# Output bias through a 33-row matmul instead of GpSimd additions in a fused attention and feed-forward kernel

## The chip, the cores and the metric

The kernel runs on one core of one Trainium2 chip. The metric is the device time of one execution in microseconds (us); lower is better. The core has TensorE (PE, with its weight loads shown apart as PEld), VectorE (DVE), ScalarE (ACT), GpSimd (POOL) and SyncE (SP, which issues the DMAs here).

## The reference

```python
# x: (8, 2048, 512); H = 16 heads of DH = 32; M = 128 features
qkv = x @ Wqkv + bqkv                      # q, k, v, split into heads
feature(t) = exp(t @ omega - 0.5 * sum(t * t))
q_prime, k_prime = feature(q), feature(k)
k_v = sum over n of k_prime^T v ; k_sum = sum over n of k_prime
attn = (q_prime @ k_v) / (q_prime @ k_sum + 1e-6)
x = layernorm(x + attn @ Wout + bout)
x = layernorm(x + x @ weight^T + pooled(x) @ disha)
```

All of it is in float32. The change is about `+ bout`, the bias of the output projection, a vector of 512 numbers that is added to every row.

## The kernel before

**Tiles.** The 8 x 2048 rows are worked in 32 chunks of 512 rows, a chunk in 4 tiles of 128 rows. Every large product is made of three float16 products that accumulate in one PSUM bank (high by high, high by low, low by high), so that a projection of one tile is 12 matmuls with a 128-row weight and 512 moving columns. Weights are scaled by WS = 16.

**Pieces.** The work is cut into pieces with two-letter names, and their order on TensorE is written out by hand in strings (`ORDER` for 28 of the 32 chunks, `ORDER_0`, `ORDER_K`, `ORDER_FIRST` ahead, `ORDER_LAST`, `ORDER_Q` behind). KP, VP, QP project keys, values, queries; KN, QN make norms; KF, QF multiply by omega (98-row weights or 98-row moving data); KV sums keys by values; KFIN finishes that sum per batch; NM is the numerator and denominator; AT transposes the attention output; WO is the output projection; YT transposes the normalized rows' input; FF is the feed-forward product; Z writes the result. A piece of 12 matmuls stands in the string in two halves (`WO1.` is the first six, `WO1` the last six), with smaller pieces between. A mark ' means the chunk before. The other engines walk the same strings in their own order: DVE with small lags or by readiness, ACT and POOL in the order in which pieces end.

**Around the change.** SP loads the bias once, spread over 128 partitions, into `bias_out` (L405), and loads the rows of x for tile t into `rows[:, t, :]` once the result that lay there has been stored. GpSimd adds `bias_out` to these rows, 128x512 float32, once per tile (`add_bias`, L958; placed in its order behind the pieces NM0, NM2, QF12 and NM4), and signals `xb_done`. GpSimd also makes rstd and shift of the second layernorm (L969, L972), for which ACT's Z waits. A WO piece: PE waits for `at_hi_done` (ACT's high part of the transposed attention output), then for the bank to be free (`bank_free`, L433), and issues the first six matmuls in `twelve` (L443 to L452); DVE then waits for `wo_done` and `xb_done` and writes rows = bank / 256 + rows (L888), from which the statistics (L770), YT (L610, transposes), ACT's `yt_hi` (L709) and DVE's `yt_lo` (L883) follow. QP, YT and AT share bank_x; WO and FF share bank_y in the long middle.

The stretch of `ORDER` that the prediction speaks of:

```
... AT0 NM2 Z3' KF0 VP1 QF8 NM3 WO0. KF1 QF9 WO0 KV0 KF2 VP2. AT1 KV1 QF10 VP2 QF11
KF3 WO1. QF12 YT0 KV2 QF13 WO1 QF14 QP3. KF4 QF15 ...
```

DVE's subtractions L818 (`k_feat_lo`), L825 (`q_feat_lo`) and L851 (`kv_lo`), the scaling L873 (`attn`) and the addition L866 (`den`) read SBUF only. L883 and L888 read PSUM and SBUF.

Of the kernel before, what the change touches and what calls it, by code (L numbers as in the profile page):

```python
# [22 lines left out]
F32 = mybir.dt.float32  # L23
# [127 lines left out]
def build(nc, xt, x, wqkv, bqk, bv, wout, bout, omega, wffn, disha, out):  # L151
    ctx = ExitStack()
    with ctx:
# [44 lines left out]
        bias_qk = sb("bias_qk", [P, 2 * G], F32)  # L198
        bias_qk16 = sb("bias_qk16", [P, 2 * G], F32)
        bias_v16 = sb("bias_v16", [P, D], F32)  # L200
        bias_out = sb("bias_out", [P, D], F32)
        omega_f = sb("omega_f", [P, M], F32)
        omega_s = sb("omega_s", [P, M], F16)
        norm_w = sb("norm_w", [P, 32], F32)
# [44 lines left out]
        def units(bank):  # L249
# [5 lines left out]
            k_hi k_sq k_lo v_hi_done v_lo_done kn_hi kn_lo k_exp kfl kfin fin_a fin_b fin_l fin_c nm_low nm_sum k_stacked  # L255
            qp_done qn_done qf_done nm_done at_done wo_done yt_done ff_done q_hi q_sq q_lo qn_hi qn_lo
            q_exp qfl q_stacked den_done rec_done normed at_hi_done at_lo_done yt_hi_done yt_lo_done
            xb_done r1_done st1 ag1 floor_done st2 ag2 var2 rstd2 z_done w_sum w_summed bv_scaled w_mean w_even pool_pow
            xt_loaded xt_hi_done xt_lo_done dve_waited sp_waited""".split()
        S = {n: sem(n) for n in names}  # L260
        xk_loaded, wk_loaded = ([sem(f"{s}_loaded{kb}") for kb in range(KB)] for s in ("xk", "wk"))
# [62 lines left out]
        def _(sp):  # L324
# [60 lines left out]
            def step(b, c, kind, i, what):  # L385
                kA, j, jq = 4 * b + c, 4 * b - 4 + c, 4 * b - 3 + c
                if kind == "XT":
                    if kA + 1 < B * CPB:
                        wait(sp, "xt_lo_done", kA)
                        if kA == 0:  # L390
                            wait(sp, "xk_lo", KB)
                        carry()
                        load_xt(kA + 1)
                elif kind == "WL":
                    if kA == 0:
                        sp.dma_start(wq_f[:, :, :], rows_of_w(wqkv, 0)).then_inc(wq_loaded, 16)
                        sp.dma_start(wo_f, rows_of_w(wout, 0)).then_inc(wo_loaded, 16)
                        sp.wait_ge(S["wk_lo"], KB)
                        sp.dma_start(wf_f, rows_of_w(wffn, 0)).then_inc(wf_loaded, 16)
                        for r in range(2):  # L400
                            sp.dma_start(attn[64 * r:64 * (r + 1), :], disha).then_inc(disha_loaded, 16)
                        sp.dma_start(bias_v16[:, :], bv.partition_broadcast(P)).then_inc(bv_loaded, 16)
                        sp.dma_start(bias_out[:, :], bout.partition_broadcast(P)).then_inc(bo_loaded, 16)
                elif kind == "STK":
                    stack_up("k", kA, "k_stacked")  # L405
                elif kind == "NRK":
                    stack_norms("k", kA, "k_stacked")
                elif kind == "STQ":
                    stack_up("q", jq, "q_stacked")
                elif kind == "NRQ":  # L410
                    stack_norms("q", jq, "q_stacked")
                elif kind == "LX":
                    load_x(b, c, i, j)
                elif kind == "ST":
                    store(b, c, i, j)
# [8 lines left out]
        def _(pe):  # L424
# [15 lines left out]
                        wait(pe, name, per * chunk_of(*there, k) + m + 1)  # L440
                        return

            def twelve(bank, parts, what, done, order, low):  # L443

                at = [(kb, *order[m]) for m in range(3) for kb in range(KB)]
                for n in (range(0, 6) if what == "first" else range(6, 12)):
                    if n == 8:
                        wait(pe, *low)
                    lhs, rhs = parts(*at[n])
                    last = nc.tensor.matmul(bank[:, :], lhs, rhs, start=n == 0, stop=n == 11)  # L450
                if what == "last":
                    last.then_inc(S[done], 1)  # L452

# [28 lines left out]
            def step(b, c, kind, i, what):  # L482
# [91 lines left out]
                elif kind == "NM":  # L574
                    t, u = i // 2, i % 2
                    wait(pe, "qfl", 16 * j + 8 * (t // 2 + 1))
                    if i < 2:
                        wait(pe, "kfin", 2 * b - 1 + i)
                    bank = bank_nm_of(b, c, i)
                    if bank is bank_kf:  # L580
                        wait(pe, "k_exp", 16 * B * CPB)
                    if alone(b, c):
                        wait(pe, "nm_sum", 8 * LAST_Q)
                        wait(pe, "normed", 8 * j + max(i - 1, 0))
                    else:
                        wait(pe, "nm_sum", 8 * j + i)
                    for hl in range(8):
                        h = 8 * u + hl
                        hh = G * (h % HPG) + h // HPG
                        pos = slice(P * (t % 2), P * (t % 2 + 1))  # L590
                        at = W1 * hl if alone(b, c) else WN * hl
                        width = WN if hl < WIDE and not alone(b, c) else W1
                        nc.tensor.matmul(bank[:, at:at + width], q_feat_hi[:, hh, pos], kv_both[:, h, 0:width],  # L593
                                         start=True, stop=False, skip_group_check=True)
                        if width == W1:
                            nc.tensor.matmul(bank[:, at:at + W1], q_feat_hi[:, hh, pos], kv_lo[:, h, :],
                                             start=False, stop=False, skip_group_check=True)
                        last = nc.tensor.matmul(bank[:, at:at + W1], q_feat_lo[:, hh, pos], kv_hi[:, h, :],  # L598
                                                start=False, stop=True, skip_group_check=True)
                    last.then_inc(S["nm_done"], 1)  # L600
                elif kind in ("AT", "YT"):
                    if kind == "AT":
                        wait(pe, "normed", 8 * j + 2 * i + 2)
                    else:
                        wait(pe, "r1_done", TPC * j + i + 1)
                    bank_free(b, c, kind, i)
                    src = attn[:, :] if kind == "AT" else rows[:, i, :]
                    bank = bank_of(b, c, kind, i)
                    for kb in range(KB):
                        last = nc.tensor.transpose(bank[:, P * kb:P * (kb + 1)],  # L610
                                                   src[:, P * kb:P * (kb + 1)], ident[:, :])
                    last.then_inc(S["at_done" if kind == "AT" else "yt_done"], 1)
                elif kind in ("WO", "FF"):
                    if what == "first":
                        wait(pe, "at_hi_done" if kind == "WO" else "yt_hi_done", TPC * j + i + 1)
                        bank_free(b, c, kind, i)
                    if j == 0 and i == 0 and what == "first":
                        wait(pe, "wo_lo", KB)
                        wait(pe, "wf_lo", KB)
                    l, r = (at_p[i % 2], wo_p) if kind == "WO" else (yt_p[i % 2], wf_p)  # L620
                    twelve(bank_of(b, c, kind, i), lambda kb, s, m: (l[s][:, kb, :], r[m][:, kb, :]), what,
                           "wo_done" if kind == "WO" else "ff_done", LHS_LOW_LAST,
                           ("at_lo_done" if kind == "WO" else "yt_lo_done", TPC * j + i + 1))

            slots(pe, PE_ORDERS, step)

# [89 lines left out]
        def _(dve):  # L716
# [79 lines left out]
            def step(b, c, kind, i, what):  # L796
# [87 lines left out]
                                    yt_hi[:, u, :, :], ALU.subtract).then_inc(S["yt_lo_done"], 1)  # L884
                elif kind == "WO":
                    wait(dve, "wo_done", n)
                    wait(dve, "xb_done", n)
                    v.scalar_tensor_tensor(out=rows[:, i, :], in0=bank_of(b, c, kind, i)[:, :], scalar=1.0 / WS / WS,  # L888
                                           in1=rows[:, i, :], op0=ALU.mult,
                                           op1=ALU.add).then_inc(S["r1_done"], 1)  # L890
# [24 lines left out]
                elif kind == "WF":  # L915
                    if kA == 2:
                        if i == 0:
                            dve.wait_ge(bv_loaded, 16)
                            v.tensor_scalar(bias_v16[:, :], bias_v16[:, :], WS, None, ALU.mult).then_inc(S["bv_scaled"], 1)
                            dve.wait_ge(wf_loaded, 16)  # L920
                            dve.wait_ge(disha_loaded, 16 * 2)
                            dve.wait_ge(S["pool_const"], 2)
                        sum_w(i)
# [22 lines left out]
        def _(pool):  # L946
# [4 lines left out]
                                    ).then_inc(S["pool_const"], 1)  # L951
            pool.wait_ge(S["dve_const"], 5)

            def add_bias(j, t):
                if j == 0:
                    pool.wait_ge(bo_loaded, 16)
                wait(pool, x_loaded[t], 16 * (j + 1))
                nc.gpsimd.tensor_tensor(rows[:, t, :], rows[:, t, :], bias_out[:, :],  # L958
                                        ALU.add).then_inc(S["xb_done"], 1)

            BIAS_BEHIND = (("NM", 0), ("NM", 2), ("QF", 12), ("NM", 4))

            def step(b, c, kind, i, what):
                kA, j = 4 * b + c, 4 * b - 4 + c
                if kind == "FF":
# [5 lines left out]
                    wait(pool, "pool_pow", TPC * j + i + 1)  # L971
                    nc.gpsimd.tensor_scalar(shift[:, u:u + 1], mean_var[:, 1, u, 0:1], rstd[:, u:u + 1], -1.0,  # L972
                                            ALU.mult, ALU.mult).then_inc(S["rstd2"], 1)
                elif (kind, i) in BIAS_BEHIND:
                    add_bias(j, BIAS_BEHIND.index((kind, i)))

            slots(pool, ENDED, step)

# [32 lines left out]
```

## Time and profile before

| | us |
|---|---|
| median of 3 runs | 2447.77 |
| lowest and highest of them | 2444.79, 2451.57 |
| the profiled execution | 2453.35 |
| its span, first to last instruction | 2451.6 |
| granted TensorE clock, mean over the span | 0.995 of full speed |

The profile is one execution. Its page gives the busy time of each engine, the chain of work that ended last, and the costliest groups of instructions by line. A matmul's end in it is modelled: matmuls that follow each other start closer together than their shown durations, so the distance of starts is what a matmul costs, and a busy TensorE is not one at its peak. For an idle stretch of PE the profile names what ended it.

### The profile page before, as it was taken

The numbers are of one execution on the slowest core, as the hardware profiler recorded it, in microseconds if no ns is written. First come the engines' busy times: TensorE is split into PE (matmuls) and PEld (weight loads), VectorE is DVE, ScalarE is ACT, GpSimd is POOL, SyncE is SP. The second block draws the span as 40 slices with busy tenths as digits, with TensorE's granted clock in tenths as the row PEclk, the third lists the DMA queues.
The fourth block names the chain that finished last, engine by engine and source line by source line (L and its number), as shares of the span: only waits on it lengthen the run. The fifth ranks groups of instructions, "written<-read, shape, count | busy, mean of one in ns | idle before, by whom it ended". The sixth has DMA issues, their size and how long they took to land.

```text
span 2451.6 us, 55233 instructions
## 1 busy us (share of the span) xinstructions
PE 2364.0 (96%) x21224; PEld 1326.1 (54%) x21224; DVE 1984.2 (81%) x4007; ACT 1265.7 (52%) x2281; POOL 291.1 (12%) x390
## 2 busy tenths in 40 slices
PE   8989999999999999999999999999999999998897
PEld 3545555555555555555555555555555555554454
DVE  6777887888888888888888888888887888877776
ACT  4544555555555555555555555555555555554433
POOL 0001111011111011111011111011111011111121
PEclk9999999999999999999999999999999999999999
DMA  6322323323323323323323323323323323221231
GB/s 204 87 69 74 102 70 91 92 77 94 101 69 94 92 72 99 96 64 104 92 68 104 93 65 102 91 72 105 79 79 97 86 81 105 73 68 53 71 91 48
DMA packets 160277, 213.11 MB, mean 87 GB/s; under 512 B 19376, under 2 KB 119824, under 8 KB 156048
## 3 DMA queue, kind: packets, MB, share of 16 engines
q1 hardware_dynamic: 159440, 208.53, 30.7%
q8 instruction: 170, 2.79, 0.5%
q10 hardware_dynamic: 576, 1.05, 0.1%
q14 instruction: 91, 0.75, 0.1%
HBM read 73.19 MB, written 33.55 MB: 44 GB/s over the span
## 4 chain that ended last, share of the span: by engine, by line
PE 61%; DVE 22%; issue 8%; ACT 5%; SPq 1%; POOL 1%; DMA 1%; DVEq 0%; POOLq 0%; ACTq 0%
PE bank_a L450 18%; PE bank_y L450 13%; PE bank_x L450 13%; DVE q_feat_lo L825 3%; DVE k_feat_lo L818 3%; PE bank_qf L569 3%; PE bank_x L610 3%; PE bank_kf L515 2%; DVE xt_lo L938 2%; DVE stats L770 2%; PE kv_ps L541 2%; DVE yt_lo L883 2%; DVE v_both L812 1%; PE bank_nm L593 1%; DVE nm_f L863 1%
## 5 line engine op out<-in xcount | busy, mean ns | idle before, releaser
L678 ACT ACTIVATE k_feat<-bank_kf 128x512 f32<-128x512 f32 x512 | 305.8, 597 | 255.1 <-PE bank_kf L515 223.8
L688 ACT ACTIVATE q_feat<-bank_qf 128x512 f32<-128x512 f32 x512 | 304.9, 595 | 177.1 <-PE bank_qf L569 176.6
L818 DVE TENSOR_TENSOR k_feat_lo<-k_feat 128x512 bf16<-128x512 f32 x512 | 369.6, 722 | 19.5 <-ACT k_feat L678 19.1
L825 DVE TENSOR_TENSOR q_feat_lo<-q_feat 128x512 bf16<-128x512 f32 x512 | 352.5, 695 | 33.2 <-ACT q_feat L688 28.7
L969 POOL TENSOR_TENSOR rstd<-mean_var,minus_half 128x1 f32<-128x1 f32 x128 | 82.8, 647 | 1687.3 <-DVE mean_var L901 1687.3
L958 POOL TENSOR_TENSOR rows<-rows,bias_out 128x512 f32<-128x512 f32 x128 | 165.9, 1308 | 456.3 <-DMA rows<-x 456.3
L515 PE MATMUL bank_kf<-omega_s,stack_k 98*128 98x128 f16 x1920 | 185.9, 219 | 3.4 <-ACT k_feat L678 3.0
L569 PE MATMUL bank_qf<-stack_q,omega_s 98*128 98x256 f16 x960 | 184.4, 273 | 4.1 <-ACT q_feat L688 3.2
L541 PE MATMUL kv_ps<-v_both,k_feat 128*128 128x65 f16 (+1 forms) x2048 | 181.4, 190 | 4.8 <-DVE k_feat_lo L818 4.8
L515 PEld LDWEIGHTS bank_kf<-omega_s,stack_k 98*128 98x128 f16 x1920 | 137.9, 97 | 85.7 <-issue 23.5
L547 PE MATMUL kv_ps<-v_both,k_feat_lo 128*128 128x33 f16 x2048 | 182.7, 179 | 0.0
L541 PEld LDWEIGHTS kv_ps<-v_both,k_feat 128*128 128x128 bf16 x2048 | 154.3, 97 | 48.6 <-DVE k_feat_lo L818 15.1
L781 DVE SCALAR_TENSOR_TENSOR t_lo_k<-bank_a,bias_qk,t_hi_k 128x512 f16<-128x512 f32 x119 | 89.3, 751 | 110.4 <-ACT squares_k L651 110.4
L704 ACT ACTIVATE at_hi<-bank_x 128x512 f16<-128x512 f32 x112 | 66.9, 597 | 206.2 <-PE bank_x L610 206.1
L781 DVE SCALAR_TENSOR_TENSOR t_lo_q<-bank_x,bias_qk,t_hi_q 128x512 f16<-128x512 f32 x128 | 95.8, 749 | 80.2 <-ACT squares_q L651 80.2
L547 PEld LDWEIGHTS kv_ps<-v_both,k_feat_lo 128*128 128x128 bf16 x2048 | 142.6, 96 | 30.8
L450 PE MATMUL bank_y<-wout_lo,at_hi 128*128 128x512 f16 x512 | 153.8, 382 | 0.0
L646 ACT ACTIVATE t_hi_q<-bank_x,bias_qk 128x512 f16<-128x512 f32 x128 | 88.1, 688 | 124.1 <-PE bank_x L450 120.7
L450 PE MATMUL bank_x<-xt_hi,wqkv_hi 128*128 128x512 f16 x512 | 132.8, 382 | 19.9 <-DVE yt_lo L883 19.2
L450 PE MATMUL bank_x<-xt_hi,wqkv_lo 128*128 128x512 f16 x512 | 148.3, 380 | 0.0
L593 PE MATMUL bank_nm<-kv_both,q_feat 128*128 128x66 bf16 (+1 forms) x1920 | 138.8, 188 | 6.6 <-issue 3.6
L598 PE MATMUL bank_nm<-kv_both,q_feat_lo 128*128 128x33 bf16 x1920 | 143.2, 178 | 0.0
(198 smaller groups left out, 5180.5 us busy)
## 6 DMA issues: line engine op xcount, KB each, us to landing
rows<-x SPq DMA_DIRECT2D x128, 256.0 KB, 2.9
out<-rows SPq DMA_DIRECT2D x128, 256.0 KB, 2.0
xt_f<-xt SPq DMA_DIRECT2D x31, 1024.0 KB, 5.1
stack_k<-t_hi_k SPq DMA_DIRECT2D x240, 128.0 KB, 2.4
stack_q<-t_hi_q SPq DMA_DIRECT2D x240, 128.0 KB, 2.4
stack_k<-t_lo_k SPq DMA_DIRECT2D x120, 128.0 KB, 2.4
stack_q<-t_lo_q SPq DMA_DIRECT2D x120, 128.0 KB, 2.4
stack_q<-t_hi_k SPq DMA_DIRECT2D x16, 128.0 KB, 2.4
```

The costliest lines, as they stand in the source:

```text
L450: last = nc.tensor.matmul(bank[:, :], lhs, rhs, start=n == 0, stop=n == 11)
L515: last = nc.tensor.matmul(bank_kf[:, M * jj:M * (jj + 1)], stack_of("k", kA)[0:STACK, g, jj, P * t:P * (t + 1)], omega_s[0:STACK, :], star ...
L541: nc.tensor.matmul(o[:, at:at + width], hi, v_both[:, t, h, 0:width], start=c == 0 and t == 0 and h % 8 == 0, stop=False, skip_group_check ...
L547: last = nc.tensor.matmul(o[:, at:at + W1], lo, v_both[:, t, h, 0:W1], start=False, stop=end, skip_group_check=True)
L569: last = nc.tensor.matmul(bank_qf[:, HALF * e:HALF * (e + 1)], omega_s[0:STACK, :], stack_of("q", j)[0:STACK, hh % G, hh // G, HALF * half ...
L593: nc.tensor.matmul(bank[:, at:at + width], q_feat_hi[:, hh, pos], kv_both[:, h, 0:width], start=True, stop=False, skip_group_check=True)
L678: nc.scalar.activation(k_feat[:, i % 2, :], bank_kf[:, :], ACT.Exp, scale=1.0 / WS).then_inc(S["k_exp"], 1)
L688: nc.scalar.activation(q_feat[:, 2 * pair:2 * pair + 2, :], bank_qf[:, :].rearrange("p (e n) -> p e n", e=2), ACT.Exp, scale=1.0 / WS).the ...
L781: v.scalar_tensor_tensor(out=t_lo[s][:, i, :], in0=bank[:, :], scalar=bias_qk16[:, m:m + 1], in1=t_hi[s][:, i, :], op0=ALU.add, op1=ALU.su ...
L818: v.tensor_tensor(k_feat_lo[:, u, :], k_feat[:, u, :], k_feat_hi[:, u, :], ALU.subtract).then_inc(S["kfl"], 1)
L825: v.tensor_tensor(q_feat_lo[:, at, :], q_feat[:, at, :], q_feat_hi[:, at, :], ALU.subtract).then_inc(S["qfl"], 1)
L958: nc.gpsimd.tensor_tensor(rows[:, t, :], rows[:, t, :], bias_out[:, :], ALU.add).then_inc(S["xb_done"], 1)
```

## The change

The bias enters the accumulation of WO on TensorE. `bias_rows` holds the float16 high part of 16 x bias (computed for 33 partitions at once; row 0 is used) and, in row 32, its low part; `pick` is a 33x128 float16 weight, zero but for rows 0 and 32, which hold 16. One matmul with this weight and 512 columns opens the accumulation of each WO bank, ahead of the twelve, whose first now has start=False. Rows 1 to 31 meet zero weights. PE waits for the free bank first, issues this matmul, and waits for `at_hi_done` behind it. GpSimd's additions and the semaphore `xb_done` are gone; DVE's L888 waits for the load of the rows itself. The set-up of the two tensors (five DVE instructions) is put once into the piece WF0 of chunk 2. The bias is loaded over 33 partitions instead of 128.

```diff
-        bias_out = sb("bias_out", [P, D], F32)
+        bias_out = sb("bias_out", [DH + 1, D], F32)
+        bias_rows = sb("bias_rows", [DH + 1, D], F16)
+        pick = sb("pick", [DH + 1, P], F16)
...
-                        sp.dma_start(bias_out[:, :], bout.partition_broadcast(P)).then_inc(bo_loaded, 16)
+                        sp.dma_start(bias_out[:, :], bout.partition_broadcast(DH + 1)).then_inc(bo_loaded, 16)
...
-            def twelve(bank, parts, what, done, order, low):
+            def twelve(bank, parts, what, done, order, low, begun=False):
...
-                    last = nc.tensor.matmul(bank[:, :], lhs, rhs, start=n == 0, stop=n == 11)
+                    last = nc.tensor.matmul(bank[:, :], lhs, rhs, start=n == 0 and not begun, stop=n == 11)
...
                 elif kind in ("WO", "FF"):
                     if what == "first":
+                        bank_free(b, c, kind, i)
+                        if kind == "WO":
+                            if j == 0 and i == 0:
+                                wait(pe, "bo_lo", 1)
+                                wait(pe, "picked", 3)
+                            nc.tensor.matmul(bank_of(b, c, kind, i)[:, :], pick[:, :], bias_rows[:, :], start=True, stop=False)
                         wait(pe, "at_hi_done" if kind == "WO" else "yt_hi_done", TPC * j + i + 1)
-                        bank_free(b, c, kind, i)
...
                 elif kind == "WO":
                     wait(dve, "wo_done", n)
-                    wait(dve, "xb_done", n)
+                    wait(dve, x_loaded[i], 16 * (j + 1))
...
                             v.tensor_scalar(bias_v16[:, :], bias_v16[:, :], WS, None, ALU.mult).then_inc(S["bv_scaled"], 1)
+                            dve.wait_ge(bo_loaded, 16)
+                            v.tensor_scalar(bias_rows[:, :], bias_out[:, :], WS, None, ALU.mult).then_inc(S["bo_hi"], 1)
+                            dve.wait_ge(S["bo_hi"], 1)
+                            v.scalar_tensor_tensor(out=bias_rows[DH:DH + 1, :], in0=bias_out[DH:DH + 1, :], scalar=WS,
+                                                   in1=bias_rows[DH:DH + 1, :], op0=ALU.mult,
+                                                   op1=ALU.subtract).then_inc(S["bo_lo"], 1)
+                            v.memset(pick[:, :], 0.0).then_inc(S["picked"], 1)
+                            dve.wait_ge(S["picked"], 1)
+                            v.memset(pick[0:1, :], WS).then_inc(S["picked"], 1)
+                            v.memset(pick[DH:DH + 1, :], WS).then_inc(S["picked"], 1)
...
-            def add_bias(j, t):
-                if j == 0:
-                    pool.wait_ge(bo_loaded, 16)
-                wait(pool, x_loaded[t], 16 * (j + 1))
-                nc.gpsimd.tensor_tensor(rows[:, t, :], rows[:, t, :], bias_out[:, :],
-                                        ALU.add).then_inc(S["xb_done"], 1)
-
-            BIAS_BEHIND = (("NM", 0), ("NM", 2), ("QF", 12), ("NM", 4))
...
-                elif (kind, i) in BIAS_BEHIND:
-                    add_bias(j, BIAS_BEHIND.index((kind, i)))
```

## Rows read from the trace of the kernel before

**Rows 1.** The page: span, busy time by engine, and the chain's shares.
```profile
span 2451.6 us, 55233 instructions
...
PE 2364.0 (96%) x21224; PEld 1326.1 (54%) x21224; DVE 1984.2 (81%) x4007; ACT 1265.7 (52%) x2281; POOL 291.1 (12%) x390
...
PE 61%; DVE 22%; issue 8%; ACT 5%; SPq 1%; POOL 1%; DMA 1%; DVEq 0%; POOLq 0%; ACTq 0%
```

**Rows 2.** PE's waits, 282 to 2205 us: waiter, awaited: us in total, times, longest.
```profile
PE bank_x L450 <- DVE yt_lo L883: 16.2, 26, 1.4
PE bank_x L610 <- DVE half_norm L792: 4.8, 26, 0.3
```

**Rows 3.** One line's instructions, whole trace: count: ns min/median/max, first and last start.
```profile
L818 DVE TENSOR_TENSOR k_feat_lo<-k_feat x512: 677/684/1781, 34.3 to 2245.5; 128x512 bf16<-128x512 f32 x171
L825 DVE TENSOR_TENSOR q_feat_lo<-q_feat x512: 674/684/1356, 163.4 to 2423.7; 128x512 bf16<-128x512 f32 x171
L873 DVE TENSOR_TENSOR attn<-nm_f,den x224: 424/425/1351, 186.9 to 2231.5; 128x256 f32<-128x256 f32 x112
L851 DVE TENSOR_TENSOR kv_both<-squares_k,kv_both x16: 432/434/1443, 182.9 to 2255.6; 128x264 bf16<-128x264 f32 x16
L883 DVE TENSOR_TENSOR yt_lo<-bank_x,yt_hi x112: 677/683/693, 207.8 to 2248.3; 128x512 f16<-128x512 f32 x112
L958 POOL TENSOR_TENSOR rows<-rows,bias_out x128: 1261/1272/1727, 187.4 to 2427.0; 128x512 f32<-128x512 f32 x128
```

**Rows 4.** Timeline ahead of QP3, one chunk, POOL, DVE and PE: start us, us.
```profile
1015.02 2.50 POOL L958 TENSOR_TENSOR rows<-rows,bias_out 128x512 f32<-128x512 f32 x2 [5.29 <-DMA rows<-x]
...
1016.49 1.58 DVE L818 TENSOR_TENSOR k_feat_lo<-k_feat 128x512 bf16<-128x512 f32 x1
...
1021.60 0.68 DVE L883 TENSOR_TENSOR yt_lo<-bank_x,yt_hi 128x512 f16<-128x512 f32 x1
...
1021.37 0.38 PE L569 MATMUL bank_qf<-stack_q,omega_s 98*128 98x256 f16 x2
1022.33 1.04 PE L450 MATMUL bank_x<-xt_hi,wqkv_hi 128*128 128x512 f16 x4 [0.58 <-DVE yt_lo L883]
```

**Rows 5.** The same place in another chunk, with the longer stall.
```profile
498.78 1.59 DVE L818 TENSOR_TENSOR k_feat_lo<-k_feat 128x512 bf16<-128x512 f32 x1
...
500.90 1.15 DVE L825 TENSOR_TENSOR q_feat_lo<-q_feat 128x512 bf16<-128x512 f32 x1
...
505.11 1.04 PE L450 MATMUL bank_x<-xt_hi,wqkv_hi 128*128 128x512 f16 x4 [1.24 <-DVE yt_lo L883]
```

**Rows 6.** Timeline of PE and PEld, an ordinary WO: full-speed distances, weights of two heights.
```profile
1010.06 1.02 PE L450 MATMUL bank_y<-wout_hi,at_hi 128*128 128x512 f16 x4
...
1010.92 0.59 PE L450 MATMUL bank_y<-wout_lo,at_hi 128*128 128x512 f16 x2
...
1011.35 0.39 PE L515 MATMUL bank_kf<-omega_s,stack_k 98*128 98x128 f16 x4
```

**Rows 7.** Timeline of the tail: a WO that waits for ACT's at_hi.
```profile
2234.07 1.04 PE L450 MATMUL bank_y<-wout_hi,at_hi 128*128 128x512 f16 x4 [0.40 <-ACT at_hi L704]
```

**Rows 8.** Timeline of DVE and PE, first attention output: AT0 waits.
```profile
191.38 1.20 DVE L873 TENSOR_TENSOR attn<-nm_f,den 128x256 f32<-128x256 f32 x1
...
192.64 0.66 PE L610 MATMUL bank_x<-ident,attn 128*128 128x128 f32 x4 [2.61 <-DVE attn L873]
```

**Rows 9.** Timeline of PE behind a batch's KFIN: NM1 inside FF3.
```profile
485.36 0.59 PE L450 MATMUL bank_y<-wffn_lo,yt_hi 128*128 128x512 f16 x2
486.02 0.19 PE L593 MATMUL bank_nm<-kv_both,q_feat 128*128 128x66 bf16 x1
```

**Rows 10.** Timeline of DVE at the piece WF0 of chunk 2.
```profile
76.51 0.42 DVE L919 TENSOR_SCALAR bias_v<-bias_v 128x512 f32<-128x512 f32 x1
...
79.00 0.75 DVE L781 SCALAR_TENSOR_TENSOR t_lo_k<-bank_a,bias_qk,t_hi_k 128x512 f16<-128x512 f32 x1 [0.55 <-ACT squares_k L651]
...
80.72 0.69 DVE L736 SCALAR_TENSOR_TENSOR wout_lo<-q_feat,wout_hi 128x512 f16<-128x512 f32 x1
```

More of the change, by code:

```diff
@@ L257, in build @@
             q_exp qfl q_stacked den_done rec_done normed at_hi_done at_lo_done yt_hi_done yt_lo_done
-            xb_done r1_done st1 ag1 floor_done st2 ag2 var2 rstd2 z_done w_sum w_summed bv_scaled w_mean w_even pool_pow
+            bo_hi bo_lo picked r1_done st1 ag1 floor_done st2 ag2 var2 rstd2 z_done w_sum w_summed bv_scaled w_mean w_even pool_pow
             xt_loaded xt_hi_done xt_lo_done dve_waited sp_waited""".split()
@@ L622, in step @@
                            "wo_done" if kind == "WO" else "ff_done", LHS_LOW_LAST,
-                           ("at_lo_done" if kind == "WO" else "yt_lo_done", TPC * j + i + 1))
+                           ("at_lo_done" if kind == "WO" else "yt_lo_done", TPC * j + i + 1), kind == "WO")
             slots(pe, PE_ORDERS, step)
```

## The prediction

> **What bounds the kernel now.** I read the page first. TensorE is shown busy for 96% of the span and carries 61% of the chain that ended last, VectorE 22% [rows 1]; GpSimd is busy for 12% and has about 1% of the chain. So TensorE's time is the time, and what is left to win are its stalls. GpSimd's 128 additions of some 1.27 us each [rows 3] are not on the chain themselves. The second view, TensorE's waits in the 26 even chunks of the middle, shows what VectorE costs it: 16.2 us in 26 waits of bank_x for `yt_lo`, one a chunk, and 4.8 us in 26 waits for `half_norm` [rows 2]. The third view, durations of single lines, tells why VectorE may be late: a line that reads SBUF alone has a median of 684 ns but a maximum of 1781 or 1356 ns, `attn` 425 against 1351, `kv_lo` 434 against 1443, while `yt_lo`, which reads PSUM and SBUF, keeps to 677 to 693 [rows 3]. The timeline says with what these slow ones coincide. Two additions ran as a pair from 1015.02 for 2.50 us; `k_feat_lo` began at 1016.49 in the second of them and took 1.58 us, 0.90 over its median. VectorE works without a pause from there to `yt_lo`, which ends at 1022.28, and QP3 begins at 1022.33 [rows 4].
>
> How long TensorE really stood: full-speed matmuls of 512 columns start 0.215 us apart (four in 1010.92 - 1010.06 = 0.86 [rows 6]), so the two 256-column matmuls of QF14 at 1021.37 were through at 1021.59, and the stall was 0.74 us, 0.16 more than the 0.58 shown, because the shown end is modelled [rows 4].
>
> **Part by part, and the sum.** The sum is made against the profiled execution of 2453.35 us (span 2451.6), which lies 5.6 above the median of 2447.77; I add the sum to the median.
>
> *Added matmuls.* 128 of them, one per tile, 512 moving columns each. At 0.215 each [rows 6] that is 27.5 us on an engine that has hardly a hole, so all of it is on the path. Its waits change places but ask for nothing that is later than before: the bank was awaited in the same place. Queued behind this earlier wait are only the WO matmuls, which need the bank anyway. The trace has no 33-row weight. Nearest is the 98-row one, whose four 128-column matmuls take 0.23 us from 1011.35 [rows 6] to the next piece: the same rate per column, with no seam at the change from 128 rows to 98. So I take 0.215. Bounds: zero, if a matmul this thin ran beside its neighbour, and 0.38 us, the shown duration of one alone, 49 us in all. Where TensorE waits for ACT's high part the new matmul slips into the wait; rows show that in the tail (0.40 us [rows 7]), and I credit one such place, -0.2.
>
> *Against a page.* The matmuls of [rows 6] follow one another at 0.215 us although each has a weight of its own, so those loads are hidden. The Trainium skill ("TensorE: Matmul & The Clock Gate", Part 3, "The mechanism") says that a weight load overlaps with matmuls in flight only when its row group differs. Strictly by that rule no load here would be hidden; the trace does not agree with it. It is taken up again in the second rival.
>
> *GpSimd's additions gone, at QP3.* What they took from VectorE there is larger than the stall: 0.90 us against 0.74 [rows 4]; in the chunk with the long stall 0.91 + 0.47 = 1.38 against 1.24 + 0.16 = 1.40 [rows 5]. A stall that goes up and down with the excess is made by it. Besides, the new matmul of WO1 stands between WO0, from which `yt_lo` descends, and QP3, and so gives VectorE 0.215 us more. So the whole stall goes: 16.2 + 26 x 0.16 = 20.4 us, and 0.8 (an estimate, the mean of these) for the 27th chunk of this kind, outside the stretch: -21.2. Bounds: 0 and -21.2. What is late next there is QF15, which needs ACT's exponential of QF14, and that moves up with QF14.
>
> *In other places.* The first attention output: `attn` took 1.20 for 0.425, and AT0 waited 2.61 us for it [rows 3, 8]: -0.8. NM1 behind KFIN, seven times: `kv_lo` up to 1.443 for 0.434 [rows 3]; two matmuls from 485.36 were through at 485.79, NM1 began at 486.02 [rows 9], so 7 x 0.23 = -1.6. Bounds of the two: 0 and -2.4.
>
> *Set-up.* Five VectorE instructions behind L919: a scaling (0.42), a subtraction as dear as L736 (0.69, since it has as many columns) and three memsets, together put at one more scaling (0.42, an estimate): 1.5 us. VectorE idles 0.55 us soon behind that place [rows 10], and more later, so most is hidden by TensorE's queued projections; if that cover is gone it costs 1.5. I take +0.5. The smaller bias load, the missing semaphore and VectorE's wait for the rows' load itself I cost at nothing: the addition could start only when the rows had landed, at 1015.02 [rows 4], so what L888 waits for now comes 1.3 us or more before what it waited for.
>
> *Sum:* 27.5 - 0.2 - 21.2 - 0.8 - 1.6 + 0.5 = **+4.2 us**; 2447.8 + 4.2 = **2452.0 us** (the profiled execution would be 2457.6). In other words, 110 of the 128 matmuls lie in the middle and give back almost exactly what the additions cost there; the end pays.
>
> **The rivals.**
> (1) *The stall at QP3 stays*, because VectorE or ACT is late for another reason and the slow `k_feat_lo` only hides it, or because the slow instructions are not GpSimd's doing. Then +4.2 + 21.2 = +25.4, 2473 us. It decides if QP3 still starts more than 0.3 us behind QF14. Against it: the two chunks of [rows 4, 5]. Chance 0.09.
> (2) *Each new matmul shows its weight load.* One seam or two more per tile: a wait stands on either side of the matmul, and what is loaded behind a wait is not always loaded ahead. I bound a seam by the 0.16 us between a matmul's own columns and its shown end: 128 x 0.1 to 128 x 0.16 is +13 to +20 on top, 2465 to 2472 us. It decides if the distance from this matmul to the first of WO is over 0.3 us. Against it: WO's first half already stands behind two waits and follows its forerunner with no seam [rows 6]. The skill's rule named above is what would make it so. Chance 0.11.
> (3) *VectorE's relief reaches farther.* It works up to 1.4 us less per chunk, and the 4.8 us of waits for `half_norm` (9 with the 0.16 each) [rows 2] may go too, with some of the 2.6 us at AT0. Then -9 - 2, 2441 us. Against it: these waits are 0.3 at the longest in every chunk, however long QP3 had stalled in it [rows 2], so VectorE has caught up by then. Chance 0.14.
> (4) *The thin matmul is nearly free*: -20 or so, 2430 us. No row speaks for it, since 98 rows cost what 128 cost. Chance 0.02.
> My own case has 0.64.
>
> **How the numbers follow.** A change under 0.3%, 7.3 us, cannot be told from none in this kernel. My case lies at +4.2 with terms that can miss by some 5 either way, so about 0.09 of its 0.64 is beyond +7.3 and 0.01 beyond -7.3; rival (3), at -6.8, falls on both sides of the bound. Faster 0.12: 0.09 of rival (3), 0.02 of rival (4), 0.01 of mine. Slower 0.29: rivals (1) and (2) with 0.20, and 0.09 of mine. Same 0.59: 0.54 of mine and 0.05 of rival (3). The range: down to 2442, which takes in rival (3) nearly, and up to 2466, the lower end of rival (2).
>
> **What would show it.** Right: GpSimd's L958 gone; `k_feat_lo` and `q_feat_lo` with maxima near 0.7 us; the waits of bank_x for `yt_lo` down from 26 to a few; 128 new bank_y matmuls 0.215 us apart from their neighbours; the chunk's period changed by 0.1 us. Wrong: new waits of PE on the free bank ahead of the new matmul; seams around it; a wait at QP3 of the old size; a period that grew by 0.8 us, or shrank.

## The result, and the profile after

The changed kernel takes 2475.65 us (median of 4 runs, 2473.32 to 2479.97) against 2449.18 us before (median of 4 runs by then): ratio 1.0118, 95% interval 1.0105 to 1.0131, 26.5 us slower. The forecast was 2452.0 us, within 2442 to 2466; it was too low by 24 us, and outside its range. The two profiled executions lie 20 us apart (2453.35, the slowest of its kernel, and 2473.32, the fastest of its own), so sums made from the traces come out smaller than the 26.5 us between the medians.

The page of the changed kernel:

```profile
span 2471.5 us, 55236 instructions
...
PE 2406.3 (97%) x21352; PEld 1339.7 (54%) x21352; DVE 1944.2 (79%) x4012; ACT 1265.3 (51%) x2281; POOL 125.1 (5%) x262
...
PE 78%; DVE 10%; issue 4%; ACT 4%; SPq 2%; POOL 1%; DMA 1%; DVEq 0%; POOLq 0%; ACTq 0%
```

Against [rows 1]: VectorE's share of the chain fell from 22% to 10%, TensorE's rose from 61% to 78%. That is what the forecast wanted of GpSimd's going. TensorE's waits in its even middle (waiter, awaited: us in total, times, longest):

```profile
PE bank_x L612 <- DVE half_norm L799: 4.4, 26, 0.2
PE bank_nm L595 <- issue: 3.6, 6, 0.6
```

The line that led in [rows 2], 16.2 us of waits for `yt_lo`, is gone altogether. The slow VectorE instructions of [rows 3] are gone too, with maxima now beside the medians (count: ns min/median/max):

```profile
L825 DVE TENSOR_TENSOR k_feat_lo<-k_feat x512: 678/684/694, 34.0 to 2260.7; 128x512 bf16<-128x512 f32 x171
L832 DVE TENSOR_TENSOR q_feat_lo<-q_feat x512: 679/684/697, 161.7 to 2442.7; 128x512 bf16<-128x512 f32 x171
L858 DVE TENSOR_TENSOR kv_both<-squares_k,kv_both x16: 432/432/434, 181.2 to 2270.8; 128x264 bf16<-128x264 f32 x16
```

So the gain came as reckoned, and the loss is in the matmul. TensorE's timeline around WO1 and QP3, to be laid beside [rows 4, 6]:

```profile
1021.63 0.39 PE L517 MATMUL bank_kf<-omega_s,stack_k 98*128 98x128 f16 x4
1021.95 0.39 PE L622 MATMUL bank_y<-bias_rows,pick 33*128 33x512 f16 x1
1022.27 1.04 PE L452 MATMUL bank_y<-wout_hi,at_hi 128*128 128x512 f16 x4
1023.14 0.59 PE L452 MATMUL bank_y<-wout_lo,at_hi 128*128 128x512 f16 x2
...
1026.17 0.39 PE L571 MATMUL bank_qf<-stack_q,omega_s 98*128 98x256 f16 x2
1026.40 1.03 PE L452 MATMUL bank_x<-xt_hi,wqkv_hi 128*128 128x512 f16 x4
```

At the end QP3 follows QF14 after 0.23 us, that is at once. Above it, the four 98-row matmuls need 0.22 us, but the 33-row one (L622) begins 0.32 after their first: a seam of 0.10. From it to the first of WO it is 0.32 us again, where 512 columns need 0.215: a second seam of 0.105. Over all 128 of them the distance behind has a median of 0.319 us, and the seam ahead is 0.083 to 0.097 us. Each bias matmul costs 0.41 us, not 0.215; 128 x 0.195 = 25 us, as much as the miss of 24 us.

### The profile page after: what moved, and what is told of

Its sections match the earlier page's. It is cut to its first block, busy times and chain, and to the rows that moved or that the text cites. A ratio compares the mean times of both kernels' runs of the same rounds, so it can differ in the third digit from the quotient of the medians.

```text
span 2471.5 us, 55236 instructions
## 1 busy us (share of the span) xinstructions
PE 2406.3 (97%) x21352; PEld 1339.7 (54%) x21352; DVE 1944.2 (79%) x4012; ACT 1265.3 (51%) x2281; POOL 125.1 (5%) x262
## 4 chain that ended last, share of the span: by engine, by line
PE 78%; DVE 10%; issue 4%; ACT 4%; SPq 2%; POOL 1%; DMA 1%; DVEq 0%; POOLq 0%; ACTq 0%
PE bank_a L452 22%; PE bank_y L452 20%; PE bank_x L452 13%; PE bank_qf L571 5%; PE bank_x L612 4%; PE bank_kf L517 3%; DVE xt_lo L955 2%; PE kv_ps L543 2%; PE bank_nm L595 2%; PE bank_y L622 2%; SPq L363 2%; PE bank_a L479 1%; POOL rstd L977 1%; DVE stats L777 1%; PE kv_ps L549 1%
## 5 line engine op out<-in xcount | busy, mean ns | idle before, releaser
L825 DVE TENSOR_TENSOR k_feat_lo<-k_feat 128x512 bf16<-128x512 f32 x512 | 350.3, 685 | 19.2 <-ACT k_feat L685 19.0
L452 PE MATMUL bank_a<-xt_hi,wqkv_lo 128*128 128x512 f16 x472 | 140.4, 379 | 0.0
L595 PEld LDWEIGHTS bank_nm<-kv_both,q_feat 128*128 128x128 bf16 x1920 | 126.5, 97 | 21.8 <-issue 11.5
```

The lines of the kernel that those rows point to most:

```text
L452: last = nc.tensor.matmul(bank[:, :], lhs, rhs, start=n == 0 and not begun, stop=n == 11)
L825: v.tensor_tensor(k_feat_lo[:, u, :], k_feat[:, u, :], k_feat_hi[:, u, :], ALU.subtract).then_inc(S["kfl"], 1)
```

## Experiments: what makes the seams

There are two theories. **S**, the shape: a weight that fills less of the array than its neighbours costs a seam on going in and on coming out. **W**, the waits: the semaphore waits on both sides keep weights from being loaded ahead.

**1. 97 rows.** Tensors and broadcast get 97 rows, nothing else:

```diff
-        bias_out = sb("bias_out", [DH + 1, D], F32)
-        bias_rows = sb("bias_rows", [DH + 1, D], F16)
-        pick = sb("pick", [DH + 1, P], F16)
+        bias_out = sb("bias_out", [97, D], F32)
+        bias_rows = sb("bias_rows", [97, D], F16)
+        pick = sb("pick", [97, P], F16)
...
-        sp.dma_start(bias_out[:, :], bout.partition_broadcast(DH + 1)).then_inc(bo_loaded, 16)
+        sp.dma_start(bias_out[:, :], bout.partition_broadcast(97)).then_inc(bo_loaded, 16)
```

> The bias weight and its moving rows get 97 rows instead of 33 (the added rows meet zero weights, the result is the same), so that the weight reaches into all four 32-row groups as the 98-row ones do; nothing else is changed. Theory S (shape): the seams of 0.09 us ahead of the bias matmul and 0.105 us behind it come with a weight that fills less of the array than its neighbours. Then both vanish: distance to the next matmul 0.215 instead of 0.319 us, 128 x 0.195 = 25 us less than the changed kernel, about 2450.5 us, ratio to before 1.000. Rival W (waits): the seams come from the semaphore waits on both sides, which keep the weights from being loaded ahead. Then nothing moves: 0.319 us, 2475.6 us, ratio 1.012.

Measured: 2449.77 us (10 runs), before 2447.48 us; ratio 1.0014 (1.0004 to 1.0024). Theory S holds, within 1 us of its 2450.5. The same place in its timeline:

```profile
1012.05 0.39 PE L517 MATMUL bank_kf<-omega_s,stack_k 98*128 98x128 f16 x4
1012.27 0.38 PE L622 MATMUL bank_y<-bias_rows,pick 97*128 97x512 f16 x1
1012.49 1.03 PE L452 MATMUL bank_y<-wout_hi,at_hi 128*128 128x512 f16 x4
```

Both seams have closed: 0.22 us ahead, 0.22 behind. A matmul with three times the rows is 0.2 us cheaper. Both waits are still in their places here, so waits alone do not make a seam.

**2. 65 rows.** The same edit with 65.

> 65 rows: three of the four row groups. Theory S in its finer forms: if the array is worked in whole, half and quarter heights, 65 rows count as the whole and the seams vanish (about 2450.5 us); if every number of row groups is a shape of its own, they stay (2475.6 us). Rival W: 2475.6 us.

Measured: 2451.3 us (10 runs); ratio 1.0015 (1.0006 to 1.0025). There are no seams:

```profile
1011.64 0.39 PE L517 MATMUL bank_kf<-omega_s,stack_k 98*128 98x128 f16 x4
1011.86 0.38 PE L622 MATMUL bank_y<-bias_rows,pick 65*128 65x512 f16 x1
1012.08 1.03 PE L452 MATMUL bank_y<-wout_hi,at_hi 128*128 128x512 f16 x4
```

**3. 64 rows.** The same edit with 64.

> 64 rows: two full row groups, no partly filled one. Theory S: the seams stay at 0.09 and 0.105 us, 2475.6 us. A rival P (a partly filled row group, the 33rd row, makes them): they vanish, 2450.5 us. Rival W: 2475.6 us.

Measured: 2476.78 us (4 runs); ratio 1.0121 (1.0099 to 1.0144). One row fewer and the seams are back:

```profile
1021.89 0.39 PE L517 MATMUL bank_kf<-omega_s,stack_k 98*128 98x128 f16 x4
1022.21 0.39 PE L622 MATMUL bank_y<-bias_rows,pick 64*128 64x512 f16 x1
1022.53 1.04 PE L452 MATMUL bank_y<-wout_hi,at_hi 128*128 128x512 f16 x4
```

The edge lies between 64 and 65 rows: 65 rows pass as full height, 64 and 33 do not. That rules out the partly filled row group, and a shape for every number of groups. Weights of 32 rows or fewer were not run.

**4. Both waits ahead of the matmul.**

```diff
                     if what == "first":
+                        wait(pe, "at_hi_done" if kind == "WO" else "yt_hi_done", TPC * j + i + 1)
                         bank_free(b, c, kind, i)
...
-                        wait(pe, "at_hi_done" if kind == "WO" else "yt_hi_done", TPC * j + i + 1)
```

> The changed kernel with TensorE's wait for at_hi_done and that for the free bank both ahead of the 33-row matmul, so that no wait stands between it and the twelve. Rival W: the seam behind it (0.105 us) goes, 13.4 us less, about 2462 us. Theory S: the seams stay, 2475.6 us, or up to 1 us more, since the few waits for ACT's high part now come ahead of the matmul.

Measured: 2475.98 us (4 runs); ratio 1.0124 (1.0106 to 1.0142), the changed kernel's time. With no wait between them the distance to WO still has a median of 0.319 us. Theory W falls here too, and with it the reason I gave for my second rival.

**5. The matmul twice, at half the weight.** Does every low weight cost, or only the change?

```diff
-                            nc.tensor.matmul(bank_of(b, c, kind, i)[:, :], pick[:, :], bias_rows[:, :], start=True, stop=False)
+                            for first in (True, False):
+                                nc.tensor.matmul(bank_of(b, c, kind, i)[:, :], pick[:, :], bias_rows[:, :], start=first, stop=False)
...
-                            v.memset(pick[0:1, :], WS).then_inc(S["picked"], 1)
+                            v.memset(pick[0:1, :], WS / 2).then_inc(S["picked"], 1)
```

(and the same for row 32.)

> The changed kernel with the 33-row matmul issued twice per tile, back to back, at half the weight (the result is the same). If a seam stands only where weights of one height follow weights of another, the second is 0.215 us behind the first, and the seams of the tile stay two: 128 x 0.215 = 27.5 us more than the changed kernel, about 2503 us. Rival: every weight under three row groups shows its load, whatever stood before it: 0.31 us between the two, 128 x 0.31 = 40 us more, about 2516 us.

Measured: 2503.77 us (4 runs); ratio 1.0222 (1.0198 to 1.0245), 28.1 above the changed kernel where 27.5 was expected for "only the change".

```profile
1020.68 0.60 PE L623 MATMUL bank_y<-bias_rows,pick 33*128 33x512 f16 x2
1021.21 1.04 PE L452 MATMUL bank_y<-wout_hi,at_hi 128*128 128x512 f16 x4
```

The pair takes 0.53 us, that is 0.32 + 0.215: the second low weight adds its columns and no seam. The seam belongs to the change of shape.

TensorE's weight loads (PEld) show where the seam stands. First the changed kernel, then the one with 97 rows, at the place shown above:

```profile
1021.95 0.09 PEld L622 LDWEIGHTS bank_y<-bias_rows,pick 33*128 33x128 f16 x1
1022.27 0.33 PEld L452 LDWEIGHTS bank_y<-wout_hi,at_hi 128*128 128x128 f16 x3 [0.23 <-issue]
```

```profile
1012.22 0.10 PEld L622 LDWEIGHTS bank_y<-bias_rows,pick 97*128 97x128 f16 x1
1012.27 0.53 PEld L452 LDWEIGHTS bank_y<-wout_hi,at_hi 128*128 128x128 f16 x3
```

With 97 rows the load for WO's first matmul begins at 1012.27, with the bias matmul, 0.22 us ahead of the matmul that uses it. With 33 rows it begins at 1022.27, with its own matmul. At the change of shape the next weight is no longer loaded ahead. Whether the 0.10 us is this load coming late or TensorE running empty first, these rows cannot tell.

The evidence had been in the trace of before. Each KN or QN piece uses 128x32 weights among wider ones; here is one in the kernel before:

```profile
1035.15 1.03 PE L450 MATMUL bank_a<-xt_lo,wqkv_hi 128*128 128x512 f16 x4
1036.11 1.07 PE L477 MATMUL bank_x<-squares_q,norm_w 128*32 128x512 f32 x8
```

Four matmuls of 512 columns are through 0.86 us after their start, at 1036.01; the narrow ones begin at 1036.11. That is the same 0.10 us, and no wait is named for it. These weights are float32 as well, but that does not make the seam: AT's float32 weights of full width follow the same matmuls at once (two in 0.43 us).

```profile
201.76 0.59 PE L450 MATMUL bank_a<-wqkv_lo,xt_hi 128*128 128x512 f16 x2
202.19 0.60 PE L610 MATMUL bank_x<-ident,attn 128*128 128x128 f32 x4
```

The Trainium skill ("TensorEngine Tiling (Array Packing)", "Key Properties") says it in a sentence: changing the tiling mode drains TensorE. The Trainium skill's list of modes (the same page, "Available Configurations") has heights of 128, 64 and 32 rows. The runs agree as far as they go: there is an edge at 64 rows, and the change costs 0.08 to 0.10 us in and 0.105 us out. That the seam is a drain, and the edge at 32 rows, no run here shows.

## Experiments: what GpSimd's additions cost

**6. No additions, no matmul** (the bias is left out).

```diff
-                nc.gpsimd.tensor_tensor(rows[:, t, :], rows[:, t, :], bias_out[:, :],
-                                        ALU.add).then_inc(S["xb_done"], 1)
+                pool.sem_inc(S["xb_done"], 1)
```

> The kernel before with GpSimd's additions left out and nothing in their place (the bias bout is not added at all); the semaphore is still counted up when the rows have landed. Theory A (my prediction): VectorE's slow instructions and with them TensorE's stall at QP3 are GpSimd's doing: k_feat_lo and q_feat_lo stay under 0.72 us, the stall is gone, 23 to 25 us less than before, about 2425 us, ratio 0.990. Rival: the slow instructions stay, or the stall moves elsewhere: 2445 to 2449 us.

Measured: 2426.58 us (4 runs), before 2448.54; ratio 0.9913 (0.9898 to 0.9928), 22.0 us less. VectorE's `k_feat_lo` keeps to its median and TensorE waits no more for `yt_lo`; the first two of TensorE's waits are now (282 to 2205 us, which here reaches past the even stretch: the 27th wait, of 1.1 us, lies behind it)

```profile
PE bank_x L610 <- DVE half_norm L792: 5.8, 27, 1.1
PE bank_nm L593 <- issue: 3.7, 6, 0.6
```

```profile
L818 DVE TENSOR_TENSOR k_feat_lo<-k_feat x512: 678/684/694, 34.2 to 2217.6; 128x512 bf16<-128x512 f32 x171
```

The slow instructions were GpSimd's doing, and their removal alone is worth nearly what the forecast said: 22.0 us, where this run was expected to give 23 to 25 and the three terms of the sum (21.2, 0.8, 1.6) make 23.6.

**7. The matmul and the additions together.** The changed kernel with GpSimd adding a tile of zeros, 128 times:

```diff
+        zeros = sb("zeros", [P, D], F32)
...
-                    wait(dve, x_loaded[i], 16 * (j + 1))
+                    wait(dve, "xb_done", n)
...
+                nc.gpsimd.tensor_tensor(rows[:, t, :], rows[:, t, :], zeros[:, :],
+                                        ALU.add).then_inc(S["xb_done"], 1)
```

> The changed kernel, with GpSimd's 128 additions put back, of a tile of zeros (the result is the same; one more memset at set-up). Both parts then stand alone: against the changed kernel it shows what the additions cost where the matmul is there, against before what the matmul costs where the additions are there. Theory A: the stall at QP3 comes back, less what the matmul of WO1 and its seams give VectorE (0.41 us): some 0.4 us per chunk and more in the long ones, +12 to +20 us on the changed kernel, 2488 to 2496 us. Rival (additions cost nothing any more): 2475.6 us.

Measured: 2480.26 us (4 runs); ratio 1.0132 (1.0114 to 1.0150), only 4.6 us above the changed kernel. I had expected 12 to 20. The stall at QP3 does not come back, though the slow instructions do. VectorE ahead of QP3, in the changed kernel:

```profile
1095.47 0.69 DVE L825 TENSOR_TENSOR k_feat_lo<-k_feat 128x512 bf16<-128x512 f32 x1
...
1097.58 0.69 DVE L819 TENSOR_TENSOR v_both<-bank_a,v_both 128x512 f16<-128x512 f32 x1 [0.22 <-ACT v_both L679]
...
1099.95 0.69 DVE L832 TENSOR_TENSOR q_feat_lo<-q_feat 128x512 bf16<-128x512 f32 x1 [0.48 <-ACT q_feat L695]
1100.56 0.68 DVE L890 TENSOR_TENSOR yt_lo<-bank_x,yt_hi 128x512 f16<-128x512 f32 x1
```

and in this run:

```profile
1095.54 1.26 DVE L826 TENSOR_TENSOR k_feat_lo<-k_feat 128x512 bf16<-128x512 f32 x1
...
1100.33 0.68 DVE L891 TENSOR_TENSOR yt_lo<-bank_x,yt_hi 128x512 f16<-128x512 f32 x1
```

With the dearer matmuls TensorE has become the slower of the two: VectorE idles 0.70 us in this stretch, behind ACT and so behind TensorE, and 0.57 us of slow `k_feat_lo` only fill that. The other chunks agree. The ten VectorE instructions up to `yt_lo` have 0.04 us of idle time between them without the matmul (experiment 6), 0.34 with the 97-row one and 0.74 with the 33-row one (medians of 27 chunks). Slow instructions lengthen them by 0.86 us in the kernel before and by 0.79 here. The additions' price is not their own; it is the slack of VectorE's run that decides. I had carried the slack of one matmul (0.215 us, WO1) and not what more of them do to the rest. The 4.6 us are not clear of noise either: the two intervals of the ratio overlap, and the even middle shows 0.03 us a chunk, 0.9 us in all. Additions beside a 97-row matmul were not run; that part of the stall would come back there, with only 0.34 us of idle time, is an argument and not measured.

**8. The additions at another time.** No matmul; the additions of tiles 2 and 3 wait until `yt_lo` of tile 0 is written:

```diff
                 wait(pool, x_loaded[t], 16 * (j + 1))
+                if t in LATE:
+                    wait(pool, "yt_lo_done", TPC * j + 1)
                 nc.gpsimd.tensor_tensor(rows[:, t, :], rows[:, t, :], bias_out[:, :],
...
+            LATE = (2, 3)
```

> The kernel before with one wait more: GpSimd's additions for tiles 2 and 3 wait until VectorE has written yt_lo of tile 0, so that they no longer meet the run of VectorE's work ahead of QP3. The bias is added as before, no matmul. Theory A: the stall at QP3 (0.79 us per chunk, 21 us in all) goes, and the additions collide with VectorE where nothing waits for it: about 2429 us, ratio 0.992. Rival: the stall only moves to the next place where TensorE waits for VectorE (the next bank_x), or the next loads: 2440 to 2455 us.

Measured: 2431.17 us (4 runs); ratio 0.9931 (0.9912 to 0.9950), 17.4 us less than before, near the 2429 expected. It beats both kernels, and the bias is added in full. Its timeline at QP3:

```profile
1008.85 0.69 DVE L883 TENSOR_TENSOR yt_lo<-bank_x,yt_hi 128x512 f16<-128x512 f32 x1
...
1009.68 2.81 POOL L960 TENSOR_TENSOR rows<-rows,bias_out 128x512 f32<-128x512 f32 x2 [11.79 <-DVE yt_lo L883]
1009.75 1.03 PE L450 MATMUL bank_x<-xt_hi,wqkv_hi 128*128 128x512 f16 x4
...
1011.89 1.15 DVE L825 TENSOR_TENSOR q_feat_lo<-q_feat 128x512 bf16<-128x512 f32 x1
```

The pair of additions now runs beside QP3 instead of ahead of it. It still slows `q_feat_lo` (1.15 us), but nothing waits there.

**9. The addition of tile 0 moved as well.**

```diff
                 wait(pool, x_loaded[t], 16 * (j + 1))
+                if t == 0:
+                    wait(pool, "normed", 2 * TPC * j + 2)
                 if t in LATE:
```

> The kernel before with the additions of tiles 2 and 3 behind yt_lo, as in the run with late additions (2431.2 us), and the addition of tile 0 behind the writing of the first tile's attention output, so that it no longer meets kv_lo behind KFIN and attn at the head. Theory A: 7 x 0.23 + 0.8 = 2.4 us less, about 2428.8 us, ratio 0.992. Rival: the later addition is awaited by VectorE's L888 of WO0 or meets other work: 2431 us or more.

Measured: 2440.45 us (9 runs), before 2448.12; ratio 0.9967 (0.9954 to 0.9980): 9 us worse than the run before it. The rival held. TensorE waits again at two places, a little in nearly every chunk:

```profile
PE kv_ps L541 <- DVE k_feat_lo L818: 4.4, 26, 0.2
...
PE bank_x L450 <- DVE yt_lo L883: 0.7, 3, 0.3
```

The second is QP3's. The profile names three of these waits, but the distance from QF14's last matmul to QP3 has a median of 0.262 us, against 0.109 in experiment 8. The period has grown by 0.24 us a chunk, 6.2 us in all; the trace's end part is 5.3 us longer and its head 3.7 us shorter (TensorE's clock stays at 2.4 GHz between 100 and 200 us, and falls to 1.2 twice in experiment 8's trace). What the moved addition meets now is a small VectorE instruction of the second layernorm:

```profile
993.19 1.27 POOL L962 TENSOR_TENSOR rows<-rows,bias_out 128x512 f32<-128x512 f32 x1 [7.59 <-DVE attn L873]
```

```profile
994.01 0.47 DVE L901 TENSOR_TENSOR mean_var<-mean_var,floor 128x1 f32<-128x1 f32 x1
```

L901 takes 0.16 us in the kernel before, always; here it is slow in 26 places of the middle, by 8.5 us in all (0.83 at the longest). That this lateness is what reaches `k_feat_lo` and `yt_lo` is read from the trace, not tested. A gain of 2.4 us had been sought at two places, and lost at places not looked at.

## Why the prediction was wrong, point by point

The start of QP3 in two of the even chunks, 26 chunks apart, gives a mean period free of the noise of the two ends:

| kernel | from, to (us) | per chunk |
|---|---|---|
| before | 282.57, 2206.19 | 73.99 |
| no additions, no matmul | 277.38, 2178.29 | 73.11 |
| matmul with 97 rows | 278.45, 2198.43 | 73.85 |
| changed (33 rows) | 280.06, 2221.29 | 74.66 |
| matmul and additions | 279.09, 2221.16 | 74.70 |
| late additions | 276.67, 2182.33 | 73.29 |

Changed against before it is 0.68 us a chunk, 17.6 of the 20 us between the two traces; the forecast had 0.1 or less.

- *The stall at QP3 goes: right.* 0.88 us per chunk less without the additions; I had 0.79, and 0.06 for NM1 (right as well: six late NM1, 1.5 us in all, are gone). The causal reading, that a stall which follows the excess of the slow instructions is made by them, was borne out. Rivals (1), (3) and (4) did not happen: the waits for `half_norm` stayed, 4.4 us after 4.8.
- *The added matmul at 0.215 us: the step that failed.* It measured 0.41, because a change of weight shape costs a seam on either side, which the sum had at nothing. With 97 rows the forecast's terms hold: 0.73 us a chunk over the kernel without either (I had 0.86; the rest went into short pauses that are there anyway, 0.09 us of it into one ahead of a QP piece), and 2449.77 us against 2447.48, +2.3 where the sum said +4.2. From 97 rows to 33 it is 0.81 us more a chunk, four times 0.2. I took the price of a 33-row weight from the 98-row one as "the nearest row". It was nearest in height and on the other side of an edge; the 128x32 weights of KN and QN, which do leave the full shape, stood in the same trace with their seam and were not read.
- *Rival (2), seams around the matmul: right in its sign and in what it looked at, wrong in its reason and a little small.* It gave 0.10 to 0.16 us per tile and 2465 to 2472 us; it was 0.195 and 2475.65. I made it hang on waits, and argued it down to a chance of 0.11 because WO's first half follows its waits with no seam. That is true, and experiments 1 and 4 show that waits have nothing to do with it. The rule of the Trainium skill that I weighed ("TensorE: Matmul & The Clock Gate", Part 3, "The mechanism") misled me too. By its sentence, loads overlap only when the row group differs; here the loads of 128-row weights behind one another were hidden at 0.215 us, and those next to a 33-row weight were not, the reverse. I had also read it too strictly: the same section of the Trainium skill names a background weight buffer, into which loads are pulled ahead, and that fits the 0.215 us of [rows 6].
- *The first attention output: a little mis-sized.* `attn` is back at 0.42 us and AT0 waits 1.62 instead of 2.61 us: 1.0 for my 0.8. But the head as a whole (up to the first times of the table) ends 5.2 us earlier without the additions, and 2.5 us earlier in the changed kernel, which has its first six dear matmuls there. Part is the clock: these windows (window: us, busy PE, PEld, DVE, ACT, POOL with counts, granted clock, DMA share, GB/s) are of the kernel before, of the changed one, and of experiment 6, without additions or matmul:

```profile
180.00:200.00 20.00, 15.44 (x125) 7.97 (x124) 14.54 (x38) 6.41 (x14) 4.94 (x4) 0.83 0.38 103
```

```profile
180.00:200.00 20.00, 16.59 (x158) 9.48 (x159) 15.39 (x42) 7.81 (x16) 0.00 (x0) 0.91 0.28 82
```

```profile
180.00:200.00 20.00, 16.43 (x166) 9.49 (x165) 17.04 (x46) 8.06 (x16) 0.00 (x0) 1.00 0.35 97
```

  The mean granted clock is 0.83 and 0.91 in the first two, a mix of the levels 1.2 and 2.4 GHz, and 1.00 in experiment 6, 2.4 GHz throughout. TensorE stands idle for 1.9 us between 179 and 184 in all three. Behind that the clock falls to 1.2 GHz in the first two, and not in experiment 6. It falls again behind AT0's wait of 2.6 us in the kernel before, but in the trace of experiment 7 it stays full behind a wait of 2.45 us there. So the length of a stall alone does not decide it, and how much of the head's gain is the additions' stays open.
- *Set-up, moved waits, smaller load: seemingly as good as nothing.* The 97-row kernel, which has them all, comes out 2 us under the sum; no run takes them apart.

## What to carry to other kernels

Before adding a small matmul to a busy TensorE, see whether its weight leaves the shape of its neighbours; among full-height weights, a bias row costs less in a weight padded with zeros to 65 rows or more than in a thin one. Where VectorE is slowed by GpSimd, ask first who waits at that place: moving two of four additions by a few microseconds gave 17.4 us, replacing all four by 33-row matmuls lost 26.5, and by 97-row ones still 2.3. And what one engine's delay costs has to be read anew once the other has more to do.

## What the runs showed of the hardware

- A 33- or 64-row weight among weights of 98 and 128 rows costs TensorE a seam of 0.08 to 0.10 us on the way in and 0.105 us on the way out; 65 and 97 rows cost nothing there, two 33-row weights in a row cost 0.01 us between them, and semaphore waits at the border change nothing. A change of width (128x32 weights) shows the same 0.10 us. At the seam the next weight's load begins with its own matmul and not 0.22 us ahead of it.
- GpSimd's 128x512 float32 addition lengthens VectorE instructions that read only SBUF by up to 1.1 us (1.781 for 0.684 us, [rows 3]), while `yt_lo`, which reads PSUM and SBUF, stays at 0.693 or less. With the additions gone, the longest `k_feat_lo` is 0.694 us. Short ones are lengthened too: L901, 0.16 us, to 0.83 in experiment 9.
